# Graph attention and expert routing: weights staged in four places and split by two engines, the last slots reordered, the last three graphs' experts in the weights' room

## Chip, core and metric

The kernel runs on one core of a Trainium2 chip. The metric is the device time of the whole kernel in microseconds (us); lower is better. The core has TensorE (PE, matmuls; its weight loads are listed as PEld), VectorE (DVE), ScalarE (ACT), GpSimd (POOL) and SyncE (SP), which here issues all transfers; they are carried out by 16 DMA engines.

## What is computed

128 graphs of 128 nodes with 512 features each. Two layers, each with a residual and a layer norm:

```python
# layer 0, per graph: attention with 16 heads of 32, adj is the bias (twice)
a = einsum('bhnd,bhmd->bhnm', q, k) * scale + (adj + adj)
p = softmax(a);  o = einsum('bhnm,bhmd->bhnd', p, v) @ Wo.T
x1 = layernorm(x + o)
# layer 1: one of 4 experts per graph
top1 = argmax(x1.mean(axis=1) @ router_w + router_b)
out = adj @ (x1 @ expert_w[top1])
y = relu(batch_norm(out, statistics over all graphs of the same expert))
result = layernorm(x1 + y)
```

## The kernel before, in words

Phase one goes through the graphs in **slots**; phase two reads back what phase one stored in DRAM (`x1_scratch`, `conv_scratch`), applies the batch norm, which needs the sums over all graphs, and writes the result.

**Precision.** A float32 product is made from three float32r products. Each operand is split: `hi` is the value rounded to float32r, `lo` what is left over. So each weight needs a rounding copy and a subtraction, 128x2048 each, before PE can use it. `mm3` then issues hi*hi, hi*lo and lo*hi.

**Slots.** In slot t, PE works on several graphs at once (`slot` in the tensor block): the scores of graph t; the q and k projections of the next pair of graphs (`project_qk`) and the v projection of graph t+2; the transposes of the softmax of graph t-1 (`turn`); adj times x1 of graph t-3; the output projection of graph t-2; the expert product of graph t-4; the router's logits of graph t-3; and p times v of graph t-1 (`times_v`). ACT, DVE, POOL and SP have slots of their own and are tied to PE's by semaphores. Slots 8 to 119 are a loop of 28 passes with four slots each; the slots before (from -2 for PE, ACT and DVE, from -4 for SP and POOL) and the slots 120 to 132 are written out, and in them the parts whose graph doesn't exist fall away. The order of the work in a slot is the order in which the code writes it.

**Start.** SP loads the weights in the order v, q, k, o into the two halves of `prob`, so that k waits until v is split and o until q is split (`w_split`). DVE does both steps of each split (L588 and L590). POOL splits x of the first pair (`split_xT`, L310 and L312), as of all others. PE waits for three split weights before its first matmul. In slots -1 to 2 DVE also splits the four experts, one per slot (`split_expert`, L601 and L603), which SP loads into `moments[:, 0:2048]` (L283) and whose two halves it writes to DRAM; at the end DVE clears `moments`.

**The expert of a graph.** The router's logits for graph b come from PE in slot b+3; six small DVE instructions make the expert's number, `expert_known` (L697 to L711). In slot b+4 SP waits for it, reads the number, and loads 1 MB of hi and 1 MB of lo of that expert (L261, L263) into the one pair of tiles `expert_hi` and `expert_lo`, as soon as the product of graph b-1 is done; PE's product of graph b follows in the same slot. Ahead of these loads in SP's slot stand the stores of x1 of graph t-3 and of conv of graph t-5.

**Softmax.** ACT does the 16 exponentials of a graph in two halves of 8: the first at the end of slot t, the second at the start of slot t+1, behind the rounding of o of graph t-1 (L542). ACT also copies the expert product out, twice (L576 and L577).

## Time and profile before

| | |
|---|---|
| median of 3 runs (2861.37 to 2863.1) | 2862.62 us |
| the profiled execution's own time | 2865.02 us |
| its span | 2863.3 us |
| PE busy | 2685.5 us (94%) |
| DVE busy | 2114.0 us (74%) |
| ACT busy | 1800.1 us (63%) |
| POOL busy | 764.1 us (27%) |
| DMA, mean rate | 188 GB/s |

The span is from the first to the last instruction that the profile shows. Busy time is time in which the engine has at least one instruction under way. It is a mean over stages that are limited by different things, so a view by stage has to say more. "Idle before, releaser" in a row is how long the engine stood still before the instruction, and what ended that.

### The profile page before, as it was taken

How to read it: one execution, taken by the hardware profiler on the slowest of the kernel's cores; microseconds unless marked ns; L12 is line 12 of the kernel's file. 1: busy time of each engine (PE TensorE's matmuls, PEld its weight loads, DVE VectorE, ACT ScalarE, POOL GpSimd, SP SyncE). 2: the span in 40 equal slices, each digit the busy share in tenths (PEclk: the TensorE clock that was granted, in tenths of full speed). 3: DMA queues.
4: the chain of work that ended last, by engine and by line, in shares of the span. 5: the costliest groups of instructions: out<-in, count | busy, mean ns of one | idle time of the engine just before them, and what ended most of it. 6: DMA issues, size and time to landing. Idle time of an engine off the chain costs nothing. (4 is left out here: it accounts for less than half of the span.)

```text
span 2863.3 us, 70552 instructions
## 1 busy us (share of the span) xinstructions
PE 2685.5 (94%) x24130; PEld 2367.4 (83%) x24130; DVE 2114.0 (74%) x3938; ACT 1800.1 (63%) x6146; POOL 764.1 (27%) x431
## 2 busy tenths in 40 slices
PE   6999999999999999999999999999999999756765
PEld 6888888888888888888888888888888888545554
DVE  6877777777777777777777777777777777628776
ACT  3666666666666666666666666666666666528777
POOL 2133323322333232233323322333233222111110
PEclk9999999999999999999999999999999999867667
DMA  5445444444454454444444544454444444459887
GB/s 214 173 181 184 160 163 179 178 159 169 183 179 158 165 183 169 164 173 183 167 162 172 183 156 170 179 183 157 164 182 178 159 170 170 162 221 336 334 326 267
DMA packets 165114, 537.82 MB, mean 188 GB/s; under 512 B 15538, under 2 KB 48306, under 8 KB 122034
## 3 DMA queue, kind: packets, MB, share of 16 engines
q1 hardware_dynamic: 165042, 536.96, 51.2%
q8 instruction: 34, 0.56, 0.1%
q14 instruction: 38, 0.31, 0.0%
HBM read 427.84 MB, written 109.05 MB: 188 GB/s over the span
## 5 line engine op out<-in xcount | busy, mean ns | idle before, releaser
L532 ACT ACTIVATE prob<-prob,neg_max 128x128 f32<-128x128 f32 x2048 | 791.9, 394 | 5.3 <-DVE abs_max L654 5.3
L336 POOL TENSOR_TENSOR norm<-norm,constants 128x1 f32<-128x1 f32 x128 | 70.6, 551 | 1462.7 <-DVE norm L688 1462.7
L532 ACT ACTIVATION_READ_ACCUMULATOR prob<-prob,neg_max 128x1 f32 x2048 | 395.2, 193 | 0.0
L326 POOL TENSOR_TENSOR moments<-moments,conv 128x1024 f32 x128 | 310.7, 2427 | 293.7 <-ACT conv L577 195.0
L518 ACT ACTIVATE qk<-bank 128x512 f32<-128x512 f32 x256 | 152.7, 597 | 369.0 <-PE bank L345 369.0
L345 PE MATMUL bank<-xT_hi,wq_hi 128*128 128x256 f32 x1024 | 303.0, 296 | 19.7 <-DVE wk_lo L590 19.0
L626 DVE SCALAR_TENSOR_TENSOR prob<-bank,adj_in 128x512 f32<-128x512 f32 x512 | 316.7, 681 | 3.6 <-PE bank L345 3.6
L643 DVE TENSOR_TENSOR prob<-prob,inv_sum 128x2048 f32<-128x2048 f32 x128 | 293.4, 2292 | 4.4
L649 DVE TENSOR_REDUCE neg_max<-prob 128x16 f32<-128x2048 f32 x128 | 291.7, 2279 | 0.0
L654 DVE TENSOR_REDUCE abs_max<-prob 128x16 f32<-128x2048 f32 x128 | 291.7, 2279 | 0.0
L345 PE MATMUL bank<-xT_hi,wq_lo 128*128 128x256 f32 x1024 | 290.8, 284 | 0.0
L345 PE MATMUL bank<-xT_hi,wk_hi 128*128 128x256 f32 x1024 | 290.3, 283 | 0.0
L345 PE MATMUL bank<-xT_lo,wk_hi 128*128 128x256 f32 x1024 | 290.2, 283 | 0.0
L345 PE MATMUL bank<-xT_lo,wq_hi 128*128 128x256 f32 x1024 | 290.2, 283 | 0.0
L345 PE MATMUL bank<-xT_hi,wk_lo 128*128 128x256 f32 x1024 | 290.2, 283 | 0.0
L312 POOL TENSOR_TENSOR xT_lo<-xT_in,xT_hi 128x1024 fp32r<-128x1024 f32 x64 | 280.7, 4386 | 5.1
L525 ACT ACTIVATE probT<-bank 128x512 f32<-128x512 f32 x512 | 264.9, 612 | 18.2 <-PE bank L400 18.0
L400 PE MATMUL bank<-ident,prob 128*128 128x128 f32 x2048 | 249.7, 276 | 21.5 <-DVE prob L643 21.5
L400 PEld LDWEIGHTS bank<-ident,prob 128*128 128x128 f32 x2048 | 236.2, 143 | 38.7 <-DVE prob L643 23.0
L551 ACT ACTIVATE v<-bank 128x512 f32<-128x512 f32 x128 | 76.5, 597 | 279.0 <-PE bank L345 279.0
L576 ACT ACTIVATE conv<-bank 128x512 f32<-128x512 f32 x128 | 76.7, 599 | 259.9 <-PE bank L345 259.9
L345 PEld LDWEIGHTS bank<-xT_hi,wq_hi 128*128 128x128 f32 x1024 | 196.4, 192 | 35.5 <-issue 19.0
(111 smaller groups left out, 6516.3 us busy)
## 6 DMA issues: line engine op xcount, KB each, us to landing
expert_hi<-expert_hi_scratch SPq DMA_DIRECT2D x128, 1024.0 KB, 5.0
expert_lo<-expert_lo_scratch SPq DMA_DIRECT2D x128, 1024.0 KB, 7.0
xT_in<-xT SPq DMA_DIRECT2D x64, 512.0 KB, 3.5
x_in<-x SPq DMA_DIRECT2D x128, 256.0 KB, 2.6
x_scratch<-x SPq DMA_DIRECT2D x128, 256.0 KB, 2.1
conv_scratch<-conv SPq DMA_DIRECT2D x128, 256.0 KB, 2.3
conv_in<-conv_scratch SPq DMA_DIRECT2D x32, 1024.0 KB, 7.2
x_in<-x_scratch SPq DMA_DIRECT2D x32, 1024.0 KB, 9.2
```

The source lines that it names most:

```text
L312: pool.tensor_tensor(xT_lo[:, par, :, :], xT_in[:, :, :], xT_hi[:, par, :, :].bitcast(F32), ALU.subtract).then_inc(x_split, 1)
L326: pool.tensor_tensor(acc, acc, conv[:, pv_mod(u, -5, 2), :, :].rearrange("p k d -> p (k d)"), ALU.add).then_inc(moments_added, 1)
L345: return pe.matmul(dst, lhsT, rhs, start=start, stop=stop)
L400: last = pe.transpose(ps_heads[c][:, h * P:(h + 1) * P], prob[:, pv_mod(u, -1, 2), HPC * c + h, :], ident[:, :])
L518: act.activation(qk[:, npar, c, :, :].rearrange("p k n -> p (k n)"), src[:, :], ACT.Copy).then_inc(qk_copied, 1)
L525: act.activation(probT[:, HPC * c:HPC * (c + 1), :].rearrange("p h n -> p (h n)"), ps_heads[c][:, :], ACT.Copy).then_inc(probT_copied, 1)
L532: last = act.activation(prob[:, par2, h, :], prob[:, par2, h, :], ACT.Exp, bias=neg_max2[:, par2, h:h + 1], scale=2.0, accum_out=row_sum[: ...
L576: act.activation(conv[:, p2, 0, :], ps_a[:, :], ACT.Copy).then_inc(conv_copied, 1)
L626: dve.scalar_tensor_tensor(out=prob[:, u % 2, h:HEADS:HPC, :], in0=ps_heads[h][:, :].rearrange("p (c m) -> p c m", c=C), scalar=HALF_SCALE ...
L643: dve.tensor_tensor(prob[:, p2, :, :], prob[:, p2, :, :], inv_sum[:, :].unsqueeze(2).to_broadcast([P, HEADS, P]), ALU.mult).then_inc(norma ...
L649: dve.tensor_reduce(neg_max2[:, u % 2, :], prob[:, u % 2, :, :], AX.X, ALU.max, negate=True).then_inc(max_found, 1)
L654: dve.tensor_reduce(abs_max[:, u % 2, :], prob[:, u % 2, :, :], AX.X, ALU.max, apply_absolute_value=True).then_inc(abs_found, 1)
```

## The change

Four things, all outside the loop of 28 passes:

- **Weights.** All four weights are loaded at once, behind the first pair's x, each into a place of its own: q and k into the halves of `prob`, v and o into `moments`. ACT rounds x of the first pair and then the weights in the order q, k, v, o; DVE makes the lo halves. POOL no longer splits the first pair. PE waits weight by weight (`w_split` 1, 2, 3) instead of for three. SP loads the first expert only after v is split, since it goes to the same place.
- **Last exponentials.** In slot 127 ACT does all 16 exponentials of graph 127, and in slot 128 the rounding of o of graph 127 comes at the end, before the copies of the expert product.
- **Order of the last slots.** On PE, slot 128 has the expert product last, behind p times v; slots 129 and later have the output projection first, then adj times x1, the router, and the expert product last. On DVE, in slot 129 the split of y of graph 126 stands behind the statistics of graph 127's x1.
- **Last experts.** The experts of graphs 125, 126 and 127 are loaded into the room of q, k and v, which no product needs any more. SP does it at the head of its slots 129 to 131, ahead of the stores, and needs no wait for the product before. PE waits for both halves at once.

The core of the diff:

```diff
@@ block.sync
-            for i, (k, w) in enumerate(zip("vqko", (wvT, wqT, wkT, woT))):
-                if i == 1:
-                    load_xT(0)
-                if i >= 2:
-                    sp.wait_ge(w_split, i - 1)
-                sp.dma_start(prob[:, i % 2, :, :].rearrange("p h m -> p (h m)"),
-                             w).then_inc(ld_w[i], 16)
+            load_xT(0)
+            for i, w in enumerate((wqT, wkT, wvT, woT)):
+                sp.dma_start(w_stage[i], w).then_inc(ld_w[i], 16)
...
             def slot(i, u, live):
                 t = i * 4 + u
+                b = t - 4
+                if isinstance(b, int) and b in last_expert:
+                    hi, lo, landed = last_expert[b]
+                    sp.wait_ge(qk_done, C * (B // 2))
+                    sp.wait_ge(v_done, B)
+                    sp.wait_ge(expert_known, b + 1)
+                    e = sp.value_load(expert_of[0:1, bass.ds(b, 1)], min_val=0, max_val=E - 1)
+                    for part, src in ((hi, expert_hi_dram), (lo, expert_lo_dram)):
+                        sp.dma_start(part[:, :, :].bitcast(F32), src[bass.ds(e, 1), :, :, :].rearrange(
+                            "e p c d -> p (e c) d")).then_inc(landed, 16)
...
+                    if e == 0:
+                        sp.wait_ge(w_split, 3)
@@ block.gpsimd
-                    if live(2 * pair):
+                    if live(2 * pair) and (not isinstance(t, int) or pair > 0):
                         split_xT(pair, (u // 2) % 2)
@@ block.tensor
-            pe.wait_ge(w_split, 3)
...
+                        if isinstance(t, int) and t == -2:
+                            pe.wait_ge(w_split, i + 1)
...
+                        if isinstance(b, int) and b in last_expert:
+                            hi, lo, landed = last_expert[b]
+                            pe.wait_ge(landed, 32)
...
+                if not isinstance(t, int) or t < B:
+                    adj_times_x1()
+                    project_out()
+                    expert_product()
+                    route()
+                    all_times_v()
+                elif t == B:
+                    adj_times_x1()
+                    project_out()
+                    route()
+                    all_times_v()
+                    expert_product()
+                else:
+                    project_out()
+                    adj_times_x1()
+                    route()
+                    expert_product()
@@ block.scalar
+            act.wait_ge(ld_xT, 16)
+            act.activation(xT_hi[:, 0, :, :], xT_in[:, :, :], ACT.Copy).then_inc(x_rounded, 1)
+            for i, k in enumerate("qkvo"):
+                act.wait_ge(ld_w[i], 16)
+                act.activation(w_hi[k][:, :, :].rearrange("p c d -> p (c d)"), w_stage[i],
+                               ACT.Copy).then_inc(w_rounded, 1)
...
+                if not isinstance(t, int) or t != B + 1:
+                    round_oT(t - 2)
+                if not isinstance(t, int) or t != B:
+                    exps(t - 1, pv_mod(u, -1, 2), HEADS // 2, HEADS)
...
-                exps(t, u % 2, 0, HEADS // 2)
+                exps(t, u % 2, 0, HEADS if isinstance(t, int) and t == B - 1 else HEADS // 2)
+                if isinstance(t, int) and t == B:
+                    round_oT(B - 1)
@@ block.vector
-            for i, k in enumerate("vqko"):
-                dve.wait_ge(ld_w[i], 16)
...
-                dve.tensor_copy(hi, stage).then_inc(w_rounded, 1)
+            dve.wait_ge(x_rounded, 1)
+            dve.tensor_tensor(xT_lo[:, 0, :, :], xT_in[:, :, :], xT_hi[:, 0, :, :].bitcast(F32),
+                              ALU.subtract).then_inc(x_split, 1)
+            for i, k in enumerate("qkvo"):
                 dve.wait_ge(w_rounded, i + 1)
...
+                last_joined = isinstance(t, int) and t == B + 1
+                if not last_joined:
+                    split_y()
...
+                    if last_joined:
+                        split_y()
```

How it moves instructions. **DVE at the start of the kernel**, where the weights' `_hi` and `_lo` are the two halves of each. Before:

```order
L588 CAST wv_hi<-prob 128x2048 [waits ld_w0]
L590 TENSOR_TENSOR wv_lo<-prob,wv_hi 128x2048 [waits w_rounded]
L588 CAST wq_hi<-prob 128x2048 [waits ld_w1]
L590 TENSOR_TENSOR wq_lo<-prob,wq_hi 128x2048 [waits w_rounded]
L588 CAST wk_hi<-prob 128x2048 [waits ld_w2]
L590 TENSOR_TENSOR wk_lo<-prob,wk_hi 128x2048 [waits w_rounded]
L588 CAST wo_hi<-prob 128x2048 [waits ld_w3]
```

and now:

```order
L645 TENSOR_TENSOR xT_lo<-xT_in,xT_hi 128x1024 [waits x_rounded]
L649 TENSOR_TENSOR wq_lo<-prob,wq_hi 128x2048 [waits w_rounded]
L649 TENSOR_TENSOR wk_lo<-prob,wk_hi 128x2048 [waits w_rounded]
L649 TENSOR_TENSOR wv_lo<-moments,wv_hi 128x2048 [waits w_rounded]
L649 TENSOR_TENSOR wo_lo<-moments,wo_hi 128x2048 [waits w_rounded]
L661 CAST expert_hi<-moments 128x2048 [waits ld_const,ld_expert,pool_ready,w_split]
```

The four roundings are gone from DVE, and the lo half of x has come to it.

**PE from the end of graph 127's output projection, slots 129 to 131**; `adjT_in,x` is adj times x1, `rw,sums` the router, `expert_hi,yT_hi` the first matmul of an expert product and `expert_lo,yT_hi` its last four. Before:

```order
L345 MATMUL bank<-wo_hi,oT_lo 128x512
L345 MATMUL bank<-expert_hi,yT_hi 128x512 [waits ld_hi,squared]
...
L345 MATMUL bank<-expert_lo,yT_hi 128x512 [waits ld_lo]
L345 MATMUL bank<-expert_lo,yT_hi 128x512 x3
L345 MATMUL bank<-rw,sums 1x4 [waits y_split]
L345 MATMUL bank<-rw,sums 1x4 x3
L345 MATMUL bank<-adjT_in,x 128x129 [waits y_split,expert_known,ld_adjT1,x1_ready]
L345 MATMUL bank<-adjT_in,x 128x129 x3
L345 MATMUL bank<-expert_hi,yT_hi 128x512 [waits ld_hi,squared]
```

and now:

```order
L360 MATMUL bank<-wo_hi,oT_lo 128x512
L360 MATMUL bank<-adjT_in,x 128x129 [waits oT_split,expert_known,ld_adjT1,x1_ready]
L360 MATMUL bank<-adjT_in,x 128x129 x3
L360 MATMUL bank<-rw,sums 1x4 [waits y_split]
L360 MATMUL bank<-rw,sums 1x4 x3
L360 MATMUL bank<-wq_hi,yT_hi 128x512 [waits ld_last0,squared]
...
L360 MATMUL bank<-adjT_in,x 128x129 [waits y_split,expert_known,ld_adjT1,x1_ready]
L360 MATMUL bank<-adjT_in,x 128x129 x3
L360 MATMUL bank<-rw,sums 1x4 [waits y_split]
L360 MATMUL bank<-rw,sums 1x4 x3
L360 MATMUL bank<-wk_hi,yT_hi 128x512 [waits ld_last1,squared]
```

The router of graph 126 stands ahead of the expert product of graph 125 (`wq_hi` holds that expert), and that of graph 127 ahead of the product of graph 126. Adj times x1 of graph 126 stands behind graph 127's output projection.

**SP at the head of slot 130.** Before:

```order
L232 DMA x_scratch<-x 128x512 [waits x1_ready]
L238 DMA conv_scratch<-conv 128x512 [waits conv_copied]
L257 TENSOR_LOAD expert_of [waits expert_known]
L257 ISA x2
L261 ISA [waits conv_done]
L261 DMA expert_hi<-expert_hi_scratch 128x2048
L263 DMA expert_lo<-expert_lo_scratch 128x2048
```

and now:

```order
L236 TENSOR_LOAD expert_of [waits expert_known,v_done,qk_done]
L236 ISA x2
L238 ISA
L238 DMA wk_hi<-expert_hi_scratch 128x2048
L238 DMA wk_lo<-expert_lo_scratch 128x2048
L245 DMA x_scratch<-x 128x512 [waits x1_ready]
L251 DMA conv_scratch<-conv 128x512 [waits conv_copied]
```

The expert's loads stand ahead of the two stores, and the wait for the product before is gone.

## Rows read from the trace of the kernel before

**Rows 1.** The trace in stretches of us: length, busy time of each engine with its instructions, granted clock, DMA share, rate
```profile
19.05:23.67 4.62, 4.62 (x22) 4.62 (x22) 3.29 (x2) 0.00 (x0) 0.84 (x1) 1.00 0.53 195
120.00:2440.70 2320.70, 2320.70 (x21832) 2058.84 (x21830) 1745.33 (x3155) 1484.13 (x5338) 687.32 (x361) 1.00 0.47 171
2440.70:2535.24 94.54, 56.27 (x413) 46.05 (x409) 43.02 (x100) 34.78 (x119) 18.65 (x11) 0.79 0.47 176
```

**Rows 2.** Timeline of SP's issues at the start: start us, length us, engine, line, operation, tiles
```profile
0.77 0.40 SPq L221 DMA_DIRECT2D prob<-wvT  x1
9.19 0.33 SPq L221 DMA_DIRECT2D prob<-wkT  x1
27.68 0.43 SPq L283 DMA_DIRECT2D moments<-expert_w  x1
```

**Rows 3.** List of DMA issues: count, size of each, median us from issue to landing
```profile
xT_in<-xT SPq DMA_DIRECT2D x64, 512.0 KB, 3.5
expert_lo<-expert_lo_scratch SPq DMA_DIRECT2D x128, 1024.0 KB, 7.0
prob<-wvT SPq DMA_DIRECT2D x1, 1024.0 KB, 4.8
prob<-wkT SPq DMA_DIRECT2D x1, 1024.0 KB, 4.7
```

**Rows 4.** Timeline of DVE at the start; idle before and its releaser in brackets
```profile
5.61 1.23 DVE L588 CAST wv_hi<-prob 128x2048 fp32r<-128x2048 f32 x1 [5.48 <-DMA prob<-wvT]
6.87 2.29 DVE L590 TENSOR_TENSOR wv_lo<-prob,wv_hi 128x2048 fp32r<-128x2048 f32 x1
9.35 1.79 DVE L588 CAST wq_hi<-prob 128x2048 fp32r<-128x2048 f32 x1 [0.18 <-DMA prob<-wqT]
11.17 4.31 DVE L590 TENSOR_TENSOR wq_lo<-prob,wq_hi 128x2048 fp32r<-128x2048 f32 x1
```

**Rows 5.** Timeline of PE, its first matmul
```profile
19.05 0.55 PE L345 MATMUL bank<-xT_hi,wq_hi 128*128 128x256 f32 x1 [19.05 <-DVE wk_lo L590]
```

**Rows 6.** Timeline of ACT in slot 128, two roundings of different length
```profile
2489.07 0.49 ACT L560 ACTIVATE yT_hi<-bank 128x384 fp32r<-128x384 f32 x1 [0.50 <-PE bank L345]
2489.45 0.27 ACT L562 ACTIVATE yT_hi<-bank 128x128 fp32r<-128x128 f32 x1
```

**Rows 7.** Timeline of POOL, the first half of the first pair's split
```profile
7.00 3.06 POOL L310 CAST xT_hi<-xT_in 128x1024 fp32r<-128x1024 f32 x1 [5.47 <-issue]
```

**Rows 8.** Timeline of DVE in slots -1 and 0
```profile
33.37 1.23 DVE L601 CAST expert_hi<-moments 128x2048 fp32r<-128x2048 f32 x1 [9.47 <-DMA moments<-expert_w]
40.49 2.48 DVE L626 SCALAR_TENSOR_TENSOR prob<-bank,adj_in 128x512 f32<-128x512 f32 x4 [3.57 <-PE bank L345]
```

**Rows 9.** Timeline of ACT in slot 127, the first copy of an expert product
```profile
2476.49 0.60 ACT L576 ACTIVATE conv<-bank 128x512 f32<-128x512 f32 x1 [2.13 <-PE bank L345]
```

**Rows 10.** Timeline of DVE in slots 128 and 129
```profile
2481.41 0.25 DVE L637 RECIPROCAL inv_sum<-row_sum 128x16 f32<-128x16 f32 x1 [2.38 <-ACT prob L532]
2506.98 0.14 DVE L711 TENSOR_SCALAR expert_of<-router 1x1 int32<-1x1 f32 x1
```

**Rows 11.** Timeline of PE in slots 128 to 131
```profile
2493.48 1.07 PE L345 MATMUL bank<-expert_lo,yT_hi 128*128 128x512 f32 x4
2497.39 1.13 PE L345 MATMUL bank<-adjT_in,x 128*128 128x129 f32 x8 [1.66 <-DVE oT_lo L617]
2502.14 0.47 PE L345 MATMUL bank<-expert_hi,yT_hi 128*128 128x512 f32 x1 [0.82 <-DMA expert_hi<-expert_hi_scratch]
2513.03 0.77 PE L345 MATMUL bank<-expert_hi,yT_hi 128*128 128x512 f32 x1 [4.62 <-DMA expert_hi<-expert_hi_scratch]
2516.58 1.91 PE L345 MATMUL bank<-expert_lo,yT_hi 128*128 128x512 f32 x4
2525.76 0.77 PE L345 MATMUL bank<-expert_hi,yT_hi 128*128 128x512 f32 x1 [7.00 <-DMA expert_hi<-expert_hi_scratch]
```

**Rows 12.** Timeline of SP, the load of graph 126's expert
```profile
2508.13 0.35 SPq L261 DMA_DIRECT2D expert_hi<-expert_hi_scratch  x1
```

More of the change, by code:

```diff
@@ L111, in graph_block_program @@
         ld_lo = sem("ld_lo")
+        ld_last = [sem(f"ld_last{i}") for i in range(3)]
         ld_xT = sem("ld_xT")
@@ L254, in slot @@
                 b = t - 4
-                if live(b):
+                if live(b) and (not isinstance(b, int) or b not in last_expert):
                     wait(sp, expert_known, b + 1)
@@ L438, in slot @@
                     wait(pe, qk_copied, C * nxt + (2 * u) % C + 1)
+                    if isinstance(t, int) and t == -2:
+                        pe.wait_ge(w_split, 3)
                     mm3(ps_a[:, :],
@@ new lines, in route @@
+                def route():
+                    b = t - 3
+                    if live(b):
+                        if isinstance(b, int) and b == 0:
+                            pe.wait_ge(ld_const, 32)
+                        wait(pe, y_split, b + 1)
+                        for c in range(C):
+                            last = mm(ps_small[0:1, P + 2:P + 2 + E], sums[:, c:c + 1],
+                                      rw[:, c, :], c == 0, c == C - 1)
+                        last.then_inc(router_done, 1)
```

144 lines of the change are left out of this document (72 added, 72 removed).

## Prediction

> **What bounds the kernel now.** I read the trace by stretches first [rows 1]. In the 2320.7 us from 120 to 2440.7, nearly the whole of phase one, PE is busy all the time at full clock while DVE is busy 1745 of them. The reader is to see that nothing but PE's own matmuls sets the time there, and the change touches none of them. What is left is the 19.05 us before PE's first matmul [rows 5], and the 94.5 us of the last slots up to phase two, in which PE is busy for 56 only. After that comes phase two, which nothing in the change touches: it moves as a block. So I ask two questions: how much earlier does PE start, and how much earlier do the last slots end? The timelines of each engine in these two places answer them.
>
> **The start.** PE's first matmul waits for DVE's third lo half, that of k, at 19.05 [rows 5]. DVE is the chain: the first weight lands at 5.6, each split is a copy of 1.23 and a subtraction of 2.29, and the third weight is only asked for at 9.19, when the first is done [rows 2, 4]. The subtraction of q took 4.31 instead of 2.29, beside POOL, which was splitting x at that time [rows 4, 7].
>
> *Landing.* v was asked for at 0.77 and landed 4.8 later, although 1.5 MB stood behind it; k landed 4.7 after its issue with nothing behind it [rows 2, 3]. So transfers land in the order of issue. v is there at 5.6 and the two after it, 1.5 MB, at 9.3 [rows 4]: 2.5 us per MB. Now x comes first, 3.5 after its issue [rows 3], at 4.3; then q at 6.8, k at 9.3, v at 11.8, o at 14.3.
>
> *Rounding on ACT.* The trace has no copy of 2048 columns on ACT. Two roundings of 384 and 128 columns took 0.49 and 0.27 [rows 6]: 0.86 ns per column more, so 2048 columns take 1.9 and x's 1024 take 1.0. From below, DVE's 1.23 bounds it; from above, DVE's subtraction of 2.29 [rows 4]. I take 1.9, since it is ACT's own slope.
>
> *Sum.* q is rounded at 8.7 and split at 11.1; k at 11.2 and 13.5; v at 13.7 and 16.0. x is split by 6.5 and hidden. PE begins at 11.2. At the low clock that it shows in its first 4.62 us (22 matmuls, 0.21 each [rows 1]) the twelve matmuls with q last until 13.8, so k is there just in time; v is wanted some 8 us after the start and is there. **PE starts 7.85 us earlier** (19.05 - 11.2).
>
> *Does the gain live on?* The next things not tied to PE are the load and split of expert 0, which before landed at 33.37, while DVE was wanted by PE's scores only at 40.49 [rows 8]: 3.6 us of room behind the split. Now the scores come at 32.6. The expert's load stands on SP behind x of pair 2, which waits for POOL's split of pair 1, whose x is now asked for at 6.5 and lands behind the weights, about 15.7. POOL's two steps beside DVE cost at most 6.2 (twice 3.1, [rows 7]), so the load goes out at 22 at the latest, lands 5.7 later by the distance it had before (27.68 to 33.37, [rows 2, 8]), and is split 3.5 after that, at 31.2. That is 1.4 before it is wanted. SP's new wait for v's split (16.0) lies behind that. I charge nothing for it and keep up to 3 us for the range. The split of v and o on DVE beside POOL can take 2 us more each, as q did; neither is wanted by PE before 19.
>
> A rule of the Trainium skill speaks against moving the copies: "ScalarE: Activation LUTs", Rules for kernel authors, has VectorE rather than ScalarE do plain arithmetic, as the faster of the two per element. The rows agree on the speed (1.23 against my 1.9). With both steps on DVE, q would be split at 10.3 and k at 13.9, and PE's k matmuls would begin at 13.9 instead of 13.8: the sum would be the same within 0.1. By that, the gain is made by the four places for staging, not by the second engine.
>
> **The last slots.** I follow the chain and give each time as it would stand on the clock of the trace of before; the start's gain is added at the end. Steps of DVE and PE under 2 us are taken over with the length that they have in slots 128 and 129 of that trace.
>
> *Exponentials.* In slot 128 DVE stands 2.38 for ACT's second eight [rows 10]. Put straight behind the first eight they cost ACT 8 x 0.39 = 3.1, of which 2.1 lie in ACT's wait for PE [rows 9]; the other 0.8 to 1.0 delay the rounding of o of graph 126 and with it DVE. Net 1.6: PE's transposes of graph 127 and all behind them come 1.6 earlier.
>
> *Slot 128.* The expert product goes behind p times v. Twelve matmuls take 2.9 (four in 1.07, the others 0.23 apart [rows 11]). So o of graph 127 is ready 4.5 earlier, but its lo half stands on DVE behind graph 126's statistics and router, which gain only 1.6, and the 0.4 that DVE waited for ACT there. PE's next work, which began at 2497.39 [rows 11], begins at 2495.3.
>
> *Slot 129.* That work is now the output projection of graph 127 (2.9, until 2498.2), then adj times x1 of graph 126 (1.1, until 2499.2). ACT's rounding 0.7 and DVE's split 0.9 follow, with graph 127's statistics (2.0 on DVE) beside them: y is split at 2501.1. Router on PE 0.3, x1's normalising 0.5 and six small DVE steps 1.1: the expert of graph 126 is known at 2502.7, where it was at 2507.1 [rows 10]. Graph 125's expert is known 1.6 earlier and loaded at once, at 2495.4; its second half goes out 0.45 later and lands 7.0 after that [rows 3], at 2502.8. Its product started at 2502.14 [rows 11] and now does at 2502.8, a little later, since both halves are waited for. It ends at 2505.7.
>
> *Slot 130.* Adj times x1 of graph 127 stands behind that product: until 2506.7. ACT does the copies of the product (1.1) first, then the rounding, until 2507.7; DVE's split until 2508.6; the router until 2510.2. SP needs 1.0 from the number to the issue (2507.1 to 2508.13 [rows 10, 12]) and the load 7.45: graph 127's expert is there at 2518.7. Graph 126's is there at 2511.2; even at the low clock (four matmuls in 1.91 [rows 11], twelve in 5.3) its product is done at 2516.5 and hides.
>
> *Sum.* The last product began at 2525.76 [rows 11] and now begins at 2518.7: **7.05 us earlier**. What follows it is the same.
>
> Both together: 14.9 us. From the profiled execution's 2865.02 us that makes 2850.1; it lay 2.4 above the median of the runs, so for the median 2862.62 - 14.9 = 2847.7.
>
> **Rivals.**
> 1. *The weights land together.* If four transfers in flight share the engines evenly, q lands when nearly all 4.5 MB have, at about 14, PE starts at 18.2, and the start gives 0.9. For it: nothing but that four were never in flight here. Against it: v's 4.8 with 1.5 MB behind it [rows 3]. Total gain 7.9: 2854.7. The Trainium skill, "DMA: Bandwidth & Descriptors", Two DMAs through the same engine are not ordered, says that nothing orders transfers across the 16 engines; the trace of before rather shows order.
> 2. *The start's gain dies on expert 0.* If its load lands no earlier than before, at 33.37, DVE is free for graph 0 at 36.9 instead of 40.49 [rows 8], and the start gives 3.6. Total 10.6: 2852.0. For it: SP's queue is in order and POOL shares the time with DVE. Against it: the 1.4 us worked out above.
> 3. *The product of graph 125 runs at the low clock*, because PE stood nearly still from 2499.2 to 2502.8. It was at full clock after 0.82 and at the low one after 4.62 of standing still [rows 11]; 3.6 with a router of 0.3 in it lies between. It costs 5.3 - 2.9 = 2.4 on the chain. Total 12.5: 2850.1. It lies within the forecast's own range.
> 4. *Slower.* DVE and POOL get into another step in the loop. A DVE instruction that met POOL's split lost 2.0 us (4.31 against 2.29 [rows 4]). If PE enters the loop with x's splits lying differently against DVE's slot, this could come back once per pair, 56 times in the 28 passes: up to 112 us, less 15, so 2960. It decides only once DVE's loss in a slot goes over its free time, (2320.7 - 1745)/120 slots = 4.8 us [rows 1]. Against it: each split starts by PE's own progress, and PE had the same step in every pass.
>
> **How the numbers follow.** Forecast, with rival 3 in it: 0.75, between 2843 and 2852. Its low end has loads that land 2 us sooner (graph 127's and graph 125's are both on the chain), its high end the low clock and 2 us of the start. Rival 1: 0.1. Rival 2: 0.1. Rival 4: 0.02. The rest, 0.03, is a stall that I don't see, worth nearly the whole gain. The range takes in rivals 1 and 2: 2842 to 2855. A measurement of this kernel can tell 0.2%, 5.7 us, from no change, so faster means under 2856.9: forecast and both rivals, with a little taken off for errors that add up, 0.91; within it 0.06; slower 0.03.
>
> **What would show it.** PE's first matmul at 11 to 12, with DVE's q half as its releaser, and no wait before the first k matmul. ACT's copies of 2048 columns at 1.9. DVE's wait for expert 0 ended before PE's scores, with PE as the releaser of graph 0's first DVE step. From 120 on (less 8) the same stretch with PE at 100%. At the end three waits of PE on DMA, for graphs 125, 126 and 127, of which only the first and last are on the chain; and about 87 us between the loop's last work and phase two instead of 94.5. The forecast is wrong if the first matmul waits for a transfer beyond 14, if PE stands still in slots 0 to 2 more than before, or if the loop's stretch changes by more than 1 us.

## The result, and the profile after

| | before | after |
|---|---|---|
| median | 2863.12 us (16 runs) | 2856.14 us (16 runs, 2851.97 to 2861.39) |
| ratio | | 0.9973, 95% interval 0.9965 to 0.9980 |
| profiled execution, own time | 2865.02 | 2856.59 |
| its span | 2863.3 | 2854.8 |
| phase two begins (DVE's first step in it) | 2535.24 | 2526.03 |
| from there to the end | 328.1 | 328.8 |

The change gains 7.0 us (5.7 to 10.0), about half of the 14.9 forecast, and 2856.14 lies 1.1 above the range. A second comparison on its own, told below, gave 10.9. In the profiled execution phase two begins 9.21 us earlier.

**The start** of the changed kernel. The trace in stretches (start:end and length in us, busy time of PE, PEld, DVE, ACT, POOL with instructions, granted clock, DMA share, GB/s), to be held against [rows 1]:

```profile
11.09:15.70 4.61, 4.61 (x21) 4.61 (x22) 4.37 (x2) 3.44 (x3) 0.00 (x0) 1.00 0.91 363
112.30:2433.00 2320.70, 2320.70 (x21832) 2058.89 (x21830) 1749.67 (x3155) 1485.02 (x5338) 676.10 (x361) 1.00 0.47 171
2433.00:2526.03 93.03, 56.05 (x412) 46.03 (x409) 44.85 (x100) 34.34 (x119) 18.65 (x11) 0.79 0.49 178
```

The loop's stretch is the same, only 7.7 us earlier: 2320.70 us with PE at 100% and the same 21832 matmuls. The third row, up to phase two, is 1.5 shorter. So in these two profiles the start gave 7.7, the last slots 1.5. The engines at the start, from their timelines (start, length, engine, line, operation, tiles, idle before and its releaser); ACT:

```profile
4.28 1.06 ACT L557 ACTIVATE xT_hi<-xT_in 128x1024 fp32r<-128x1024 f32 x1 [2.23 <-DMA xT_in<-xT]
6.71 1.91 ACT L560 ACTIVATE wq_hi<-prob 128x2048 fp32r<-128x2048 f32 x1 [1.38 <-DMA prob<-wqT]
9.20 1.91 ACT L560 ACTIVATE wk_hi<-prob 128x2048 fp32r<-128x2048 f32 x1 [0.58 <-DMA prob<-wkT]
```

DVE, which answers to [rows 4, 8]:

```profile
8.65 2.29 DVE L649 TENSOR_TENSOR wq_lo<-prob,wq_hi 128x2048 fp32r<-128x2048 f32 x1 [2.06 <-ACT wq_hi L560]
11.14 2.29 DVE L649 TENSOR_TENSOR wk_lo<-prob,wk_hi 128x2048 fp32r<-128x2048 f32 x1 [0.19 <-ACT wk_hi L560]
13.62 2.29 DVE L649 TENSOR_TENSOR wv_lo<-moments,wv_hi 128x2048 fp32r<-128x2048 f32 x1 [0.19 <-ACT wv_hi L560]
...
27.41 1.23 DVE L661 CAST expert_hi<-moments 128x2048 fp32r<-128x2048 f32 x1 [8.46 <-DMA moments<-expert_w]
...
32.78 2.48 DVE L686 SCALAR_TENSOR_TENSOR prob<-bank,adj_in 128x512 f32<-128x512 f32 x4 [1.81 <-PE bank L360]
```

PE, its first matmul [rows 5]:

```profile
11.09 0.55 PE L360 MATMUL bank<-xT_hi,wq_hi 128*128 128x256 f32 x1 [11.09 <-DVE wq_lo L649]
```

x landed at 4.28, q at 6.71, k at 9.20 (v and o followed at 11.68 and 14.19): in the order of issue, 2.5 us per MB. ACT's copy takes 1.91. PE begins at 11.09 instead of 19.05 and has no wait before k's matmuls. Expert 0 is there at 27.41, and graph 0's first step on DVE waits for PE, not for expert 0. Expert 1 is later than PE's need: DVE waits 1.07 for its load in slot 1, and graph 1's first step comes only 6.55 earlier than before (44.52 against 51.07). With graph 2's (62.00 against 69.69) the start's gain is whole again.

Of the 7.96 at the first matmul 7.7 are left by the first copy of PE's result on ACT (16.59 against 24.29). PE's first matmuls of 256 columns follow each other at 0.21 us, the later ones at 0.12. The slow ones lasted 4.62 before (22 of them) and 5.26 now (24).

**The last slots.** To compare with before, add 7.7. PE, to be held against [rows 11]:

```profile
2488.43 0.50 PE L360 MATMUL bank<-wo_hi,oT_hi 128*128 128x512 f32 x1 [0.77 <-DVE oT_lo L677]
...
2494.32 0.34 PE L360 MATMUL bank<-rw,sums 128*1 128x4 f32 x8 [1.94 <-DVE yT_lo L730]
2496.87 0.76 PE L360 MATMUL bank<-wq_hi,yT_hi 128*128 128x512 f32 x1 [2.21 <-DMA wq_lo<-expert_lo_scratch]
...
2501.78 1.05 PE L360 MATMUL bank<-adjT_in,x 128*128 128x129 f32 x8
2504.59 0.34 PE L360 MATMUL bank<-rw,sums 128*1 128x4 f32 x8 [1.76 <-DVE yT_lo L730]
2506.42 0.48 PE L360 MATMUL bank<-wk_hi,yT_hi 128*128 128x512 f32 x1 [1.49 <-DMA wk_lo<-expert_lo_scratch]
...
2515.70 0.77 PE L360 MATMUL bank<-wv_hi,yT_hi 128*128 128x512 f32 x1 [6.23 <-DMA wv_lo<-expert_lo_scratch]
...
2519.25 1.91 PE L360 MATMUL bank<-wv_lo,yT_hi 128*128 128x512 f32 x4
```

SP's issues there:

```profile
2488.57 0.34 SPq L238 DMA_DIRECT2D wq_hi<-expert_hi_scratch  x1
2489.01 0.38 SPq L238 DMA_DIRECT2D wq_lo<-expert_lo_scratch  x1
2489.43 0.42 SPq L245 DMA_DIRECT2D x_scratch<-x  x1
2489.91 0.64 SPq L251 DMA_DIRECT2D conv_scratch<-conv  x1
...
2507.50 0.35 SPq L238 DMA_DIRECT2D wv_hi<-expert_hi_scratch  x1
```

And the stretches around the three products (last columns: granted clock, DMA share, GB/s):

```profile
2492.40:2496.87 4.47, 0.34 (x8) 0.27 (x9) 3.04 (x14) 0.66 (x2) 0.55 (x1) 0.74 0.98 331
2496.87:2501.78 4.91, 4.91 (x13) 3.85 (x13) 0.00 (x0) 0.00 (x0) 0.00 (x0) 0.55 0.95 314
...
2506.42:2509.40 2.98, 2.98 (x12) 2.15 (x12) 0.26 (x2) 0.00 (x0) 0.00 (x0) 1.00 0.26 78
...
2515.70:2521.20 5.50, 5.45 (x12) 3.77 (x12) 0.00 (x0) 0.01 (x1) 0.00 (x0) 0.50 0.00 1
```

Graph 125's expert comes 8.3 us after its issue, and its product then takes 4.91 us at a granted clock of 0.55, where graph 126's takes 2.98 at 1.00. Behind it on PE stands graph 127's adj times x1 (2501.78), so the delay goes straight into graph 127's number and load. Graph 127's own expert comes 8.2 after its issue, PE having stood still for 6.23, and that product too is at the low clock, 5.5 us long.

PE's stretch at the head of slot 128, adj times x1 of graph 125 and the output projection of graph 126, before and after:

```profile
2487.72:2491.66 3.94, 3.94 (x21) 3.41 (x21) 0.89 (x4) 1.25 (x3) 0.00 (x0) 0.94 0.00 0
```

```profile
2478.62:2483.47 4.85, 4.85 (x21) 3.98 (x20) 0.89 (x4) 1.25 (x3) 0.00 (x0) 0.77 0.00 0
```

The same work took 0.9 longer, at a lower granted clock.

One more thing stands on the chain, on DVE. Its timeline, at the end of slot 127's work and at graph 127's number:

```profile
2471.03 1.74 DVE L699 SCALAR_TENSOR_TENSOR inv_sum<-abs_max,inv_sum 128x16 f32<-128x16 f32 x1
...
2505.15 0.14 DVE L767 TENSOR_REDUCE router<-router 1x1 f32<-1x4 f32 x1
2505.33 0.84 DVE L769 SCALAR_TENSOR_TENSOR router<-router 1x4 f32<-1x4 f32 x1
...
2506.57 0.14 DVE L778 TENSOR_SCALAR expert_of<-router 1x1 int32<-1x1 f32 x1
```

and POOL's:

```profile
2470.40 2.34 POOL L341 TENSOR_TENSOR moments<-moments,conv 128x1024 f32 x1 [3.17 <-ACT conv L637]
...
2503.82 2.34 POOL L341 TENSOR_TENSOR moments<-moments,conv 128x1024 f32 x1 [9.72 <-ACT conv L637]
```

Before, L699's step took 0.18 and L769's 0.21. Now each ends within 0.03 us of the end of POOL's addition beside it (2472.77 and 2472.74; 2506.17 and 2506.16). L699's step takes 1.73 or 1.74 in all ten profiles here with the sixteen exponentials in slot 127, and 0.17 or 0.18 in the other four: it is an effect of moving the exponentials, which brings this step under POOL's addition.

**The ledger**, each term as forecast on the clock of before, and as measured (trace of after plus 7.7):

| step of the last slots | forecast | measured | lost here |
|---|---|---|---|
| graph 125's load issued | 2495.4 | 2496.3 | 0.9 |
| both halves there | 7.45 later | 8.30 later | 0.85 |
| its product | 2.9 | 4.91 | 2.0 |
| from there to graph 127's issue | 5.5 | 5.7 | 0.2 |
| graph 127's expert there | 7.45 later | 8.20 later | 0.75 |
| its product, against 4.6 before | same | 5.5 | 0.85 |

The sum is 5.55, which is what lies between 7.05 and 1.5.

The first row is the exponentials' 1.6. Graph 125's number, which was to be known 1.6 earlier, is known 0.6 earlier. On DVE, before and now (add 7.7):

```profile
2495.89 0.14 DVE L711 TENSOR_SCALAR expert_of<-router 1x1 int32<-1x1 f32 x1
```

```profile
2487.61 0.14 DVE L778 TENSOR_SCALAR expert_of<-router 1x1 int32<-1x1 f32 x1
```

L699's step took 1.56 out of what the exponentials gave, and the slower stretch at the head of slot 128 another 0.9. Counted from graph 126's first step on DVE, the number comes 0.0 to 0.6 earlier than before in all ten profiles with the new order, so this is not one execution's chance.

### The profile page after: what moved, and what is told of

Its sections match the earlier page's. It is cut to its first block and busy times, and to the rows that moved or that the text cites. A ratio compares the mean times of both kernels' runs of the same rounds, so it can differ in the third digit from the quotient of the medians.

```text
span 2854.8 us, 70556 instructions
## 1 busy us (share of the span) xinstructions
PE 2683.5 (94%) x24130; PEld 2366.5 (83%) x24130; DVE 2114.7 (74%) x3935; ACT 1810.0 (63%) x6151; POOL 747.6 (26%) x429
## 5 line engine op out<-in xcount | busy, mean ns | idle before, releaser
L703 DVE TENSOR_TENSOR prob<-prob,inv_sum 128x2048 f32<-128x2048 f32 x128 | 304.5, 2379 | 4.4
L327 POOL TENSOR_TENSOR xT_lo<-xT_in,xT_hi 128x1024 fp32r<-128x1024 f32 x63 | 268.9, 4269 | 5.0
```

Source lines behind the costliest of these rows:

```text
L327: pool.tensor_tensor(xT_lo[:, par, :, :], xT_in[:, :, :], xT_hi[:, par, :, :].bitcast(F32), ALU.subtract).then_inc(x_split, 1)
L703: dve.tensor_tensor(prob[:, p2, :, :], prob[:, p2, :, :], inv_sum[:, :].unsqueeze(2).to_broadcast([P, HEADS, P]), ALU.mult).then_inc(norma ...
```

## The experiments

The theory formed from that: the start is worth its 7.7 us; the last slots lose theirs to (a) PE's wait for both halves at once, (b) the low clock in the products of graphs 125 and 127, and (c) the place of graph 125's product ahead of graph 127's adj times x1. Rivals: the start's gain is partly lost again in the loop; the new order is itself no gain; the loads into the weights' room are what is slow.

How far can one profile be trusted? With the same code, executions differ in slot 4 (18.1 or 19.8 us from graph 3's to graph 4's step on DVE, with and without the old start), and phase two took from 324.8 to 331.6 us. So in the profiles "phase two begins" is the mark, good to some 2 us, and the medians are the check. A closer mark for the last slots alone is the **last stretch**, from graph 126's first step on DVE to phase two. Before, it begins here:

```profile
2442.11 2.47 DVE L626 SCALAR_TENSOR_TENSOR prob<-bank,adj_in 128x512 f32<-128x512 f32 x4
```

and in the changed kernel here:

```profile
2434.42 2.47 DVE L686 SCALAR_TENSOR_TENSOR prob<-bank,adj_in 128x512 f32<-128x512 f32 x4
```

so it took 93.13 us before and takes 91.61 now. Between graph 5's first step on DVE and graph 126's lie 2316.9 to 2317.1 us in every profile here, so nothing of the start is lost or won in the loop. Four executions with the same last slots (the change, after_again, dve_both, last_only) have a last stretch of 90.3 to 91.6. All runs (times in us; each before is of the same session):

| kernel | median | before | ratio, 95% interval | phase two begins | last stretch, against 93.13 |
|---|---|---|---|---|---|
| start_only | 2855.96 | 2864.89 | 0.9970 (0.9959 to 0.9981) | 2529.34 | 92.95 (-0.2) |
| last_only | 2861.67 | 2864.89 | 0.9988 (0.9979 to 0.9997) | 2534.84 | 90.31 (-2.8) |
| dve_both | 2857.05 | 2864.89 | 0.9968 (0.9956 to 0.9980) | 2526.50 | 91.47 (-1.7) |
| hi_first | 2851.12 | 2864.89 | 0.9952 (0.9938 to 0.9965) | 2520.50 | 86.29 (-6.8) |
| order_only | 2858.70 | 2863.92 | 0.9980 (0.9971 to 0.9989) | 2529.87 | 92.99 (-0.1) |
| filled | 2855.11 | 2863.92 | 0.9970 (0.9959 to 0.9980) | 2523.93 | 90.16 (-3.0) |
| early_y | 2850.56 | 2863.92 | 0.9952 (0.9939 to 0.9966) | 2518.88 | 85.37 (-7.8) |
| early_y_hi_first | 2849.28 | 2863.92 | 0.9949 (0.9935 to 0.9962) | 2518.60 | 84.02 (-9.1) |
| room_only | 2866.56 | 2864.72 | 1.0008 (0.9999 to 1.0017) | 2537.81 | 101.41 (+8.3) |
| after_again | 2853.85 | 2864.72 | 0.9958 (0.9944 to 0.9971) | 2527.33 | 90.78 (-2.4) |
| filled_short | 2856.58 | 2864.72 | 0.9966 (0.9952 to 0.9979) | 2524.25 | 87.83 (-5.3) |
| room_hi_first | 2857.49 | 2864.57 | 0.9975 (0.9966 to 0.9983) | 2528.28 | 94.32 (+1.2) |

**start_only: the new start, everything in the last slots as before.** The order, the exponentials, the split of y and the loads are undone:

```diff
-        last_expert = {B - 3 + i: (w_hi[k], w_lo[k], ld_last[i]) for i, k in enumerate("qkv")}
+        last_expert = {}
...
-                if not isinstance(t, int) or t < B:
...
+                adj_times_x1()
+                project_out()
+                expert_product()
+                route()
+                all_times_v()
```

> The new start alone; the last slots are those of the kernel before. The traces say that the start gave 7.7 us and the last slots 1.5. Theory A (the start is the whole of the gain and lives on through the loop): PE's first matmul at 11.1 us, graph 0's first DVE step 7.7 us earlier, phase two 7.7 us earlier (2527.5), time 7 to 8.5 us under the kernel before. Theory B (the start's gain is partly an effect of the new last slots, or lost in the loop): under 5 us.

It gains 8.9 us (5.4 to 11.7). Phase two begins 5.9 earlier than before: 7.9 at the first matmul (11.19), 7.4 at graph 3's first step on DVE, less 1.6 in slot 4, where the granted clock was 0.91 in this execution and 1.00 in the changed kernel's. last_only lost 1.7 there with the old start, so it doesn't belong to the change. The last stretch is that of before.

**last_only: the old start with the new last slots.** The start's parts of the diff are undone in all engines.

> The new last slots alone, with the start as before. Theory A: phase two 1.5 us earlier than before (2533.7), time 0.5 to 2.5 us under the kernel before. Theory B (the 7 us that I forecast are there and something else in the changed kernel hides them): 5 us or more under it. The product of graph 125 is expected at the low clock, 4.9 us long.

3.2 us (0.9 to 6.0). Phase two begins 0.4 earlier in the profile, which has lost 2.3 by graph 5 (most of it in slot 4); the last stretch is 2.8 shorter. The last slots give a small part of what was forecast, whatever the start; the product of graph 125 ran at the low clock here too.

**dve_both: copies back on DVE, four places kept.**

```diff
+            dve.wait_ge(ld_xT, 16)
+            dve.tensor_copy(xT_hi[:, 0, :, :], xT_in[:, :, :]).then_inc(x_rounded, 1)
...
             for i, k in enumerate("qkvo"):
+                dve.wait_ge(ld_w[i], 16)
+                dve.tensor_copy(w_hi[k][:, :, :].rearrange("p c d -> p (c d)"), w_stage[i]).then_inc(w_rounded, 1)
                 dve.wait_ge(w_rounded, i + 1)
```

> The changed kernel, with the roundings of x and of the four weights back on DVE. My sum says that q is split at 10.3 and k at 13.9 instead of 11.1 and 13.4, so that PE starts 0.8 earlier and stands 1.0 before k: the same within 0.3 us at graph 0's first DVE step, and the same time as the changed kernel within 1 us. The rival, that the second engine makes the gain: graph 0's step 2 us or more later than in the changed kernel, since x also takes two steps on DVE.

PE's two waits at the start of this kernel, from its timeline:

```profile
10.66 0.55 PE L360 MATMUL bank<-xT_hi,wq_hi 128*128 128x256 f32 x1 [10.66 <-DVE wq_lo L646]
14.03 0.58 PE L360 MATMUL bank<-xT_hi,wk_hi 128*128 128x256 f32 x1 [0.47 <-DVE wk_lo L646]
```

PE begins 0.43 sooner, waits 0.47 for k, and graph 0's first step on DVE stands at 33.14 instead of 32.78 (in the kernels with ACT's help it lies between 31.90 and 33.21). In the end it is 2857.05, as the kernel with ACT's help: it is not the second engine that gains. What the rest of the new start is worth part by part (the four places, x and q first, PE's wait weight by weight, POOL without the first pair) no run separates. The row of wv_lo bounds one part: had PE still waited for three weights, it would have begun when v's low half is ready, at 15.91, so by this estimate 4.8 of the 7.96 hang on the wait weight by weight.

**hi_first: PE waits for the high half, and for the low one only ahead of the last four matmuls of a product.**

```diff
-                            pe.wait_ge(landed, 32)
+                            pe.wait_ge(landed[0], 16)
...
+                        else:
+                            pe.wait_ge(landed[1], 16)
```

> The changed kernel, but PE waits for the hi half of the last three experts first and for the lo half only before the last four matmuls, as the kernel before does. Theory A (waiting for both halves at once costs most of the missing gain): graph 125's product ends when its lo half has landed plus four matmuls, about 3 us earlier, the same for graph 127's, so phase two 5.5 to 7 us earlier than in the changed kernel (2519.5 to 2520.5) and the time as much lower. Theory B (the clock and the loads themselves cost it): under 2 us.

PE's timeline of it:

```profile
2497.17 1.20 PE L360 MATMUL bank<-wq_lo,yT_hi 128*128 128x512 f32 x4 [0.29 <-DMA wq_lo<-expert_lo_scratch]
2498.20 1.05 PE L360 MATMUL bank<-adjT_in,x 128*128 128x129 f32 x8
...
2511.09 0.77 PE L360 MATMUL bank<-wv_hi,yT_hi 128*128 128x512 f32 x1 [1.79 <-DMA wv_hi<-expert_hi_scratch]
```

The product of graph 125 goes on straight behind the router, at full clock, and waits only 0.29 for its low half: adj times x1 of graph 127 begins at 2498.20 instead of 2501.78. The last product still begins at the low clock. Phase two begins 5.5 us earlier than in the changed kernel, and the median is 13.8 below before. This is (a), with part of (b) in it.

**early_y: adj times x1 of graph 127 and its router in slot 129, ahead of graph 125's product;** its y goes to the room of the first pair's x, and SP loads its expert ahead of the store of conv.

```diff
-                else:
+                elif t == B + 1:
                     project_out()
                     adj_times_x1()
                     route()
+                    adj_times_x1(B - 1)
+                    route(B - 1)
+                    expert_product()
+                else:
                     expert_product()
```

> The changed kernel, with adj times x1 and the router of graph 127 ahead of graph 125's product (y of graph 127 gets a place of its own, in xT's, and SP issues its expert's load ahead of graph 125's conv store). Theory A (the number of graph 127's expert is the chain, and graph 125's product stood in it): the number is known at about 2500.5 instead of 2506.6, its expert lands at about 2509.5, behind graph 126's, and phase two comes 5 to 6.5 us earlier (2519.5 to 2521). Theory B (transfers are the bound at the end): the last load lands no earlier than 2513, and phase two comes less than 3 us earlier.

PE's timeline:

```profile
2495.22 1.63 PE L369 MATMUL bank<-adjT_in,x 128*128 128x129 f32 x8 [1.29 <-DVE expert_of L798]
...
2505.21 0.47 PE L369 MATMUL bank<-wk_hi,yT_hi 128*128 128x512 f32 x1 [1.68 <-DMA wk_lo<-expert_lo_scratch]
...
2510.99 0.47 PE L369 MATMUL bank<-wv_hi,xT_hi 128*128 128x512 f32 x1 [2.75 <-DMA wv_lo<-expert_lo_scratch]
```

Graph 127's number is known at 2499.86 instead of 2506.57, PE waits at most 2.75 at once, and the last two products run at full clock (3.0 each). Graph 125's ran at the low clock (4.7), but nothing waits for it any more. Phase two begins 7.1 earlier than in the changed kernel, more than the 5 to 6.5 expected, and the median is 13.4 below before: taking (c) away is worth as much as splitting the wait. Two smaller things are in it: SP issues the last load ahead of a store, and the DVE step in front of graph 127's number that POOL held for 0.84 takes its usual 0.21 here.

**early_y_hi_first: both at once.** No new edit.

> Both of the last two edits that take something off the chain: graph 127's y early, and the hi halves waited for first. If they add up as far as the transfers allow: the last product ends 1.5 to 2 after the last lo half lands at about 2509.5, so phase two at 2516 to 2518, 8 to 10 us earlier than in the changed kernel and 16 to 18 earlier than in the kernel before. If the transfers bound both: no better than the better one of the two alone (hi first: 2520.5).

They do not add up. The last two products in PE's timeline say why:

```profile
2506.24 0.50 PE L369 MATMUL bank<-wk_hi,yT_hi 128*128 128x512 f32 x1 [1.18 <-ACT conv L656]
...
2510.48 0.49 PE L369 MATMUL bank<-wv_hi,xT_hi 128*128 128x512 f32 x1 [1.17 <-ACT conv L656]
```

Phase two begins 0.6 after the 2518 expected at the latest. Now each product waits for ACT's copies of the one before it, since all expert products use one PSUM bank. At 2849.28 us (0.9949) this is the fastest kernel here, but not distinguishable from early_y.

**filled: PE kept at work with matmuls that nobody reads**, 15 in slot 129 around the router and 23 ahead of the last product. The kernel does this extra work; all else is as in the change.

```diff
+                    if t == B + 1:
+                        fill(7)
                     route()
+                    if t == B + 1:
+                        fill(8)
+                    if t == B + 3:
+                        fill(23)
                     expert_product()
```

> The changed kernel with 38 matmuls of 128x512 more on PE, whose results nobody reads: 7 and 8 in the two waits before graph 125's product and 23 in the wait before graph 127's. Theory A (the low clock after a wait costs what the lists show): graph 125's product starts at the same time and takes 2.9 instead of 4.9, graph 127's takes 2.9 instead of 5.4, phase two 3.5 to 4.6 us earlier (2521.5 to 2522.5). Theory B (the length of a product is not from the clock): no gain, or a loss if the added matmuls outlast the waits.

The stretch of graph 125's product in it, with its granted clock:

```profile
2496.26:2499.13 2.87, 2.87 (x12) 2.33 (x13) 0.00 (x0) 0.00 (x0) 0.00 (x0) 1.00 0.81 283
```

2.87 us instead of 4.91, as the forecast had it. The last product ran at full clock too, but the 23 matmuls ahead of it had outlasted its load by some 2.6 us. Phase two begins 2.1 earlier, where 3.5 to 4.6 were expected; by the medians it is no better than the change.

**filled_short** has 6 instead of 23 there, in one session with **after_again**, the changed kernel once more.

> As the filled kernel, but with 6 instead of 23 added matmuls before graph 127's product, since 23 outlasted the wait by about 2.6 us. Theory A (the clock is the price): graph 125's product 2.9 long, graph 127's begins when its lo half has landed, 8.2 after the issue, and is 2.9 to 3.5 long; phase two 3 to 4.5 us earlier than in the changed kernel of the same runs. Theory B: graph 127's product 4.6 or longer all the same, phase two at most 2.5 earlier.

> The changed kernel once more, on the chip of these runs, to see how far one profile of it differs from another. Theory (TensorE's clock comes up at another moment in every execution and moves single stretches by up to 2 us, and everything else repeats): first matmul at 11.1 to 11.3, time of the rise between 3 and 6 us after it, phase two at 2525 to 2529, graph 125's product starting 8.2 to 8.4 after its load's issue and graph 127's as well.

after_again came as expected but for one load: graph 125's product starts 8.27 after the issue, graph 127's 7.83.

In filled_short graph 127's product took 3.1 us, in after_again 5.5; graph 125's took 2.9 and 4.4. Phase two begins 3.1 earlier than in after_again: (b) is there, 1.6 us at graph 125 and 2.4 at graph 127, of which about 1 is lost again (graph 127's load took 8.30 instead of 7.83, and the step held by POOL ahead of it 1.32 instead of 0.84). But the median is 2.7 above after_again's, with overlapping intervals, so that filling gains time in the whole is not shown. In filled_short graph 126's product ran at the low clock (as it did in filled), which hides.

**order_only: the new order, but the last experts loaded as before into the one pair of tiles.** Against the change: `last_expert = {}`.

> The changed kernel without the loads into the weights' room: the last three experts go into the one pair of tiles, as before, with the hi half waited for first; start and order of the last slots as changed. Theory A (waiting for both halves gives back what the early loads win): the load of graph 127 goes out only at about 2510, when graph 126's product is done, but its product ends 1.5 after the lo half has landed, at 2518.5; phase two at 2523 to 2524.5, that is 1.5 to 3 us EARLIER than in the changed kernel (2526.0). Theory B (the early loads are worth something as they are): phase two later than 2526.

Missed: phase two at 2529.87, 5.4 to 6.9 later than I had it; slot 4 took the longer 19.8 in this execution and accounts for 1.6 of that. SP's issues in this kernel:

```profile
2492.46 0.35 SPq L274 DMA_DIRECT2D expert_hi<-expert_hi_scratch  x1
...
2503.00 0.35 SPq L274 DMA_DIRECT2D expert_hi<-expert_hi_scratch  x1
...
2515.18 0.34 SPq L274 DMA_DIRECT2D expert_hi<-expert_hi_scratch  x1
```

I had counted on the separate wait for the high half and overlooked that each load into the one pair of tiles now waits for a product which stands later in its slot than before. The order, with the exponentials, gains nothing over start_only: the last stretches are 92.99 and 92.95. The exponentials by themselves were not run.

**room_only: the old order, with loads into the weights' room.** Only the order, the exponentials and the split of y are undone.

> The changed kernel with the last slots in the order of the kernel before; the new start and the loads into the weights' room stay. Theory A (the wait for both halves gives away more than the early loads bring): graph 127's number is known as late as before, its load goes out 1 us after that, and its product ends 13.4 after the issue instead of 9.5; phase two 1 to 4 us later than the kernel before less the start's 7.7, so at 2528.5 to 2531.5, and the time 4 to 7 us under the kernel before. Theory B (the room is worth something by itself): phase two before 2527.

Missed again, further: no faster than before (+1.8 us, -0.3 to +4.9) in spite of the new start, and 8.5 behind start_only. PE's timeline:

```profile
2499.10 0.47 PE L360 MATMUL bank<-wq_hi,yT_hi 128*128 128x512 f32 x1 [2.39 <-DMA wq_lo<-expert_lo_scratch]
...
2512.77 0.76 PE L360 MATMUL bank<-wk_hi,yT_hi 128*128 128x512 f32 x1 [7.95 <-DMA wk_lo<-expert_lo_scratch]
...
2527.56 0.77 PE L360 MATMUL bank<-wv_hi,yT_hi 128*128 128x512 f32 x1 [10.19 <-DMA wv_lo<-expert_lo_scratch]
```

I had put one or two of these waits on the chain; in the old order all three are, since there the router of graph 126 stands behind the product of graph 125, and that of graph 127 behind the product of graph 126: each number waits for the load before it.

**room_hi_first: the same, with hi_first's wait.** It decides whether the wait or the loads cost those 8.5.

> The changed kernel with the last slots in the old order, the loads going into the dead weights, and each product waiting for the high half first and for the low half only ahead of its second part. The theory: with the old order all three loads stand on the chain that ends phase one, and waiting for both halves at once costs about 3 us at each. Then phase two begins 8 to 9 us earlier than in the same kernel with the common wait (2537.8), at 2528.5 to 2530.5, which is where the kernel with the start alone has it (2529.3). The rival: what is slow is the loads themselves (where they go, or what stands ahead of them on SyncE), and not the wait; then phase two begins less than 4 us earlier, after 2534.

```profile
2505.25 0.77 PE L360 MATMUL bank<-wk_hi,yT_hi 128*128 128x512 f32 x1 [4.00 <-DMA wk_hi<-expert_hi_scratch]
...
2517.94 0.76 PE L360 MATMUL bank<-wv_hi,yT_hi 128*128 128x512 f32 x1 [6.91 <-DMA wv_hi<-expert_hi_scratch]
```

Phase two begins 9.5 us earlier than in room_only, and the medians say 9 (ratios 0.9975 and 1.0008); 1.6 of the 9.5 is slot 4, and the last stretch is 7.1 shorter. From the issue of each load to the end of its product it took 11.4, 12.8 and 13.6 us in room_only and takes 9.8, 10.4 and 10.4 here: the common wait, with what it does to the clock, costs 1.7, 2.3 and 3.2 us at the three loads. The high halves land 4.9 to 5.0 after their issue, against 4.9 for graph 126's and 127's before, so the loads are no slower for going into the weights' room. And without an order that uses it, the room gives nothing: the last stretch is 1.4 longer than start_only's.

## Why the prediction was half right

**The start was right, in size and in its steps.** 7.96 us at the first matmul against 7.85, 7.7 of them still there in slot 0 and from slot 2 on. In slot 1 it is 6.55: DVE waits 1.07 for expert 1's load, which the prediction, looking at expert 0 alone, didn't ask about; it costs nothing in the end. The landing times hold within 0.1, ACT's copy is 1.91 against 1.9, k is just in time, and expert 0's load went out at 21.61 against "22 at the latest" and landed 5.8 later. Rival 1, the weights landing together, is refuted by ACT's rows: landing times are 2.5 apart. Rival 2, the gain dying on expert 0, by DVE's: it has 1.81 us free before graph 0's step. Rival 4, the loop in another step, by the stretch of 2320.70 us. The prediction takes PE's first 4.62 us for the low clock, while the granted clock in that row is 1.00; the spacing of the matmuls bears the prediction out, 0.21 there and 0.12 later.

**The second engine is worth nothing that can be measured**, as was worked out from the rows: dve_both's median is within 1 us of the change's 2856.14. That the four places make the gain, as the prediction says, is not shown: PE's wait weight by weight is worth more than half of it by the estimate above. The Trainium skill's rule in "ScalarE: Activation LUTs", Rules for kernel authors, gives relu, max, min, add and mul to VectorE as the faster engine per element; taken to cover a copy, it would have the copies stay on DVE. The trace agrees on the speed of the copy (1.23 against 1.91), and the runs say that it doesn't matter here.

**The last slots were wrong: 1.5 us for 7.05** (1.5 to 2.8 over four executions of the same last slots). The steps that failed are in the ledger, and they are terms of the sum, each mis-sized in the same direction, on a chain that was otherwise as described:
- *"Net 1.6"* for the exponentials. Graph 125's number came 0.6 earlier, not 1.6, and 0.0 to 0.6 in all profiles with the new order. *"Steps of DVE and PE under 2 us are taken over with the length that they have"* is why: moved earlier, a step of 0.18 fell beside POOL's addition and took 1.74, and another 0.9 went at the lower clock at the head of slot 128. A second step, 0.21 long, took 0.84 on the way to graph 127's number.
- *"Its product ... ends at 2505.7"*, 2.9 us. It took 4.91: rival 3 came true, at 2.0 of its 2.4. PE stood nearly still for 4.47 us there, not 3.6. I had held the time that PE stood still against two waits of before, and left the full clock in the sum though no row lay between them. filled shows the cause: with PE at work ahead of it the product takes 2.87.
- *"Lands 7.0 after that"*. That median is of loads in the loop. Here both took 8.2 to 8.3 from the first issue to the product, where 7.45 was in the sum, with the stores of x1 and conv issued behind graph 125's (7.4 to 8.3 in after_again and last_only). Why they are longer was not tested.
- *"What follows it is the same."* The last product took 4.6 before, its last four matmuls at full clock (1.10), and 5.5 now, these four too at the low clock (1.91).

The wait for both halves is not among these steps: the sum had it in, as the 7.45 from issue to product. Counted from issue to the end of graph 127's product it made 9.5 us before (2520.90 to 2530.36) into 13.7 now (2507.50 to 2521.16), because before the high half's matmuls ran while the low half was still on its way. The prediction paid this price, named it only as "a little later" at graph 125, and didn't ask what a split wait would give. hi_first shows it: 5.5 us more than the change.

What was not seen at all is the order's weak place: graph 125's product stands ahead of graph 127's adj times x1, so that any delay of the first load is paid at the last one. The parts of the change in the last slots depend on each other, by the last stretches: the order with the exponentials gains 0.1, the room alone loses 8.3, together they give 1.5 to 2.8. With the wait split (hi_first) or graph 127's y ahead (early_y) they give 6.8 and 7.8, about what had been forecast for a kernel with neither.

What stays open: the second comparison of the same kernel gave 10.9 us where the first gave 7.0. Their intervals (0.9965 to 0.9980 and 0.9944 to 0.9971) overlap, between gains of 8.3 and 10.0 us, and executions of one kernel differ by 9 us. 2853.85 lies within the stated range, where 2856.14 does not; but the terms above failed in both profiles: in after_again the last stretch is 2.4 shorter, graph 125's product takes 4.4 and the last one 5.5. The size of the whole is open by some 3 us, the account of the last slots is not.

## What to carry to other kernels

When a wait for two transfers is joined into one, cost it from issue to the end of the consumer, and cost the split wait beside it: the first half of the work used to run under the second transfer. A small step that is moved in time may fall beside another engine's long one and take on its length; look what runs there. A product that begins after a wait of a few us should be priced at both clocks, and on a chain the upper price is the forecast. Where loads get room of their own, look which other work stands behind the consumer in the same queue; moving that ahead was worth as much as the room.

## What the hardware showed

- **A tiny DVE instruction can be held by POOL until POOL is done.** 0.18 and 0.21 us steps with two inputs from SBUF took 1.74 and 0.84 and ended with POOL's 2.34 us addition; a reduction with one input between them (L767) took its usual 0.14 while that addition ran. The Trainium skill, "SBUF — State Buffer", section "SBUF: two separate sides", describes the port pair that the two share as an exclusive lock, which a DVE instruction with two SBUF inputs needs against a GpSimd instruction that reads SBUF; the trace agrees to 0.03 us.
- **PE's clock fell after a wait of only 2.2 us** (granted 0.55 afterwards, the lower level of 1.2 GHz for most of the product), where the wait followed on a router of 0.34 and another wait of 1.94. A wait of 1.49 behind a denser stretch left it at 1.00. With nearly the same gap (2.16), after_again's product took 4.42 (2499.02 to 2503.44). In hi_first, where no wait followed the router, the same product ran at full clock.
- **The granted clock of a row can miss a slow start.** In the first 4.62 us of PE before, and the first 4.61 now, it stands at 1.00, while matmuls of 256 columns follow each other at 0.21 us instead of the later 0.12.
- **1 MB and 2 MB from DRAM.** The high half landed 4.9 to 5.0 us after its issue in room_hi_first (2488.36, 2500.32 and 2512.96 to 2493.25, 2505.25 and 2517.94), graph 125's low half 3.7 after its high one (2496.91).
